# The squares of the first layer's output on VectorE instead of GpSimd

## What is computed

```python
x = x + _L0_xattn_ref(_layernorm(x), ctx_1024, Wq, bq, Wk, bk)
x = x + _L0_ffn_ref(_layernorm(x), w_fc, w_proj)
x = x + _L1_xattn_ref(_layernorm(x), fside, ctx_1024)
x = x + _L1_ffn_ref(_layernorm(x), Wq, keys, e_down, e_up)
```

```python
for s in SHRINKS:                                   # 16 scales
    scale = base * s
    deq = jnp.clip(jnp.round(wb / scale), -QMAX, QMAX) * scale
    err = jnp.sum((deq - wb) ** 2, axis=-1, keepdims=True)
    ... keep the scale of the least err
h = jnp.maximum(turbo_linear(x, w_fc), 0.0)         # 1024 hidden features
return turbo_linear(h * h, w_proj)
```

## Time and profile before

| | us |
|---|---|
| median of 3 runs | 459.7 |
| lowest and highest | 458.96 and 460.38 |
| the profiled execution | 458.2 |
| its span in the trace | 456.4 |

### The profile page before, as it was taken

How to read it: one execution, slowest core, us unless ns; L and a number is a source line. 1 busy time by engine, 2 the same in 40 slices (tenths; PEclk the granted TensorE clock), 3 DMA queues, 4 the chain that set the end, 5 groups by cost and what they waited for, 6 DMA issues and landing times.

```text
span 456.4 us, 6956 instructions
## 1 busy us (share of the span) xinstructions
PE 374.5 (82%) x2510; PEld 283.6 (62%) x2510; DVE 360.9 (79%) x878; ACT 248.4 (54%) x371; POOL 196.8 (43%) x211
## 2 busy tenths in 40 slices
PE   2987897599799988988388679978799878789486
PEld 1554664244345448987267568867688667688475
DVE  4998699958986956267947977698969799999991
ACT  4789959789788880136555254675475645012000
POOL 2355844479889993000011441353523325414220
PEclk9998999989989998998759968999999999979799
DMA  9910000000000004000000000000000000000000
GB/s 264 362 53 2 0 1 0 0 2 0 0 2 0 0 2 159 27 2 0 0 2 1 0 1 1 1 12 1 13 0 14 1 1 14 1 13 0 2 24 11
DMA packets 11138, 11.32 MB, mean 25 GB/s; under 512 B 608, under 2 KB 10592, under 8 KB 11104
## 3 DMA queue, kind: packets, MB, share of 16 engines
q1 hardware_dynamic: 11104, 10.88, 7.4%
HBM read 9.83 MB, written 1.05 MB: 24 GB/s over the span
## 4 chain that ended last, share of the span: by engine, by line
DVE 38%; PE 35%; ACT 13%; issue 9%; POOL 4%; DMA 1%; DVEq 0%; POOLq 0%; ACTq 0%
PE pair L728 6%; PE pair L559 5%; DVE arena L1480 5%; PE pair L697 5%; POOL arena L332 3%; PE pair L519 3%; PE pair L715 3%; PE pair L668 3%; PE pair L497 2%; PE pair L526 2%; DVE arena L1223 2%; DVE arena L1477 1%; DVE arena L1495 1%; PE pair L397 1%; DVE i L1422 1%
## 5 line engine op out<-in xcount | busy, mean ns | idle before, releaser
L332 POOL TENSOR_TENSOR arena<-arena 128x512 f32<-128x512 f32 x64 | 91.0, 1432 | 52.0 <-ACT arena L930 21.5
L697 PE MATMUL pair<-arena,EDT 128*128 128x256 f32 x256 | 59.5, 384 | 3.0 <-ACT arena L1063 3.0
L728 PE MATMUL pair<-EU,arena 128*128 128x256 f32 x256 | 57.8, 380 | 2.8 <-DVE arena L1502 1.6
L1223 DVE TENSOR_REDUCE arena<-arena 128x16 f32<-128x512 f32 x64 | 42.7, 679 | 20.2 <-POOL arena L332 20.1
L519 PE MATMUL pair<-QP,nidentr 128*128 128x512 f32 x144 | 47.6, 456 | 12.5 <-ACT arena L930 9.9
L369 POOL TENSOR_TENSOR arena<-arena,ctxT 128x2048 bf16<-128x2048 bf16 x8 | 34.8, 4351 | 46.9 <-DVE arena L1471 39.6
L697 PEld LDWEIGHTS pair<-arena,EDT 128*128 128x128 f32 x256 | 47.7, 191 | 9.9 <-ACT arena L1063 3.6
L728 PEld LDWEIGHTS pair<-EU,arena 128*128 128x128 f32 x256 | 47.9, 190 | 9.2 <-DVE arena L1495 3.1
L715 PE MATMUL pair<-arena 128*128 128x64 bf16 x768 | 30.4, 203 | 18.8 <-DVE arena L1495 9.4
L519 PEld LDWEIGHTS pair<-QP,nidentr 128*128 128x128 f32 x144 | 27.3, 203 | 24.4 <-issue 16.6
L1063 ACT ACTIVATE arena<-pair 128x512 f32<-128x512 f32 x32 | 18.7, 595 | 42.0 <-PE pair L697 41.9
(11 more groups left out here) (196 smaller groups left out, 686.1 us busy)
## 6 DMA issues: line engine op xcount, KB each, us to landing
arena<-in_L_ffn_e_down_dram SPq DMA_DIRECT2D x1, 2048.0 KB, 12.2
EU<-in_L_ffn_e_up_dram SPq DMA_DIRECT2D x1, 2048.0 KB, 8.1
arena<-in_L_ffn_w_fc_dram SPq DMA_DIRECT2D x2, 512.0 KB, 5.3
X<-in_x_dram SPq DMA_DIRECT2D x1, 1024.0 KB, 6.0
arena<-in_L_ffn_w_proj_dram SPq DMA_DIRECT2D x1, 1024.0 KB, 13.7
GUW<-in_fside_BxS2xS_dram SPq DMA_DIRECT2D x1, 1024.0 KB, 11.4
out_dram<-arena SPq DMA_DIRECT2D x8, 128.0 KB, 1.7
CTX<-in_ctx_dram SPq DMA_DIRECT2D x1, 512.0 KB, 5.0
```

Source lines behind the costliest of these rows:

```text
L332: pool.tensor_tensor(qf(g), sq[:, :, 0:32], sq[:, :, 32:64], ALU.add).then_inc(s["folded"], 1)
L697: last = pe.matmul(bk2(4 + i % 2)[:, r, :], EDT[:, k, at:at + P], xT4[:, b % 2, k, :], start=(k == 0), stop=(k == 1))
L728: last = pe.matmul(bk2(7)[:, n, :], PR[:, n, e, :], EU[:, e, :], start=(e == 0), stop=(e == EROWS - 1))
L1223: dve.tensor_reduce(err[:, g // NS % 2, :, g % NS], qf(g), AX.X, ALU.add).then_inc(s["reduced"], 1)
```

## The change

`square_hidden` is taken out of GpSimd's program and put into VectorE's, with the same operands and the same semaphores. In VectorE's loop it stands in iteration 31 + 2i behind `sum_error` of unit 28 + 2i and ahead of `choose`, `quantise`, `dequantise`, `prepare` and `scale_weights` of the same iteration.

```diff
@@ GpSimd's program
-            def square_hidden(i):
-
-                m, half = i // 2, i % 2
-                pool.wait_ge(s["f1_e"], i + 1)
-                pool.tensor_tensor(h2T[:, m, half * 512:half * 512 + 512], hr[:, i % 2, :], hr[:, i % 2, :],
-                                   ALU.mult).then_inc(s["hsq"], 1)
-
...
                 if g % NS == 12 and g // NS + 1 < NCH:
                     split(g // NS + 1)
-                if g - 2 in FFN1_UNIT:
-                    square_hidden(FFN1_UNIT[g - 2])
@@ VectorE's program
+            def square_hidden(i):
+
+                m, half = i // 2, i % 2
+                dve.wait_ge(s["f1_e"], i + 1)
+                dve.tensor_tensor(h2T[:, m, half * 512:half * 512 + 512], hr[:, i % 2, :], hr[:, i % 2, :],
+                                  ALU.mult).then_inc(s["hsq"], 1)
+
...
                     dve.tensor_reduce(m_w2[:, :], ctxT[:, :].rearrange("p (b t) -> p b t", b=B), AX.X, ALU.max,
                                       apply_absolute_value=True)
+                if g - 2 in FFN1_UNIT:
+                    square_hidden(FFN1_UNIT[g - 2])
                 for b in range(B):
                     if g == 7 + b // 2:
```

## The result

| | median, us | lowest to highest | runs |
|---|---|---|---|
| before | 459.63 | 456.59 to 460.74 | 6 |
| after | 463.92 | 463.23 to 466.18 | 6 |

The changed kernel takes 1.0112 times as long (95% interval 1.0073 to 1.0150), some 4 to 5 us more; a second time, on another chip, it was 1.0155 times (1.0102 to 1.0209). It is slower, as forecast.

A forecast was written before the change was run, and what follows sets the result against it. VectorE was taken to decide when the stage passes 125 and 161 us, GpSimd its end. 3.1 + 5.0 + 1.6 - 1.15 - 1.5 = +7.0 us, added to the median of 459.7: 466.7 us, range 461.0 to 470.0.

The forecast's parts named there:

- What bounds the stage: From 98 to 173 us: VectorE decides when the stage passes 125 and 161 us, GpSimd decides its end.
- The price of one square: On VectorE: 0.69 us plus a turn of up to 1.25 us, waiting out a GpSimd fold.
- the milder rival: Squares take no turn, only 0.69 us and the wait for the relu: +2 us, 461.7 us; chance 0.17.
- First hole, +3.1: TensorE's wait from 122.2 to 125.11 us grows 3.1 us: order 3.2, two squares 1.4, less 1.5 of waits.
- second hole, +5.0: TensorE's 0.26 us wait before 161.17 us grows 5.0 us: choose(2) 2.2 later, squares 1.4, further waits 1.4.
- the third term: Waits from choose to the end of dequantise: 1.5 us fewer at the first hole, 1.4 more at the second.
- the replay: VectorE's queue gone through operation by operation, with turns against GpSimd; gave choose(1) 3.2 us later, choose(2) 2.2.
- The clock, +1.6: Behind the second hole the granted clock falls, so TensorE's sequence takes 1.6 us more; bounds 0 and 1.6.
- The end, -1.15 and -1.5: Before ffn2, the wait for GpSimd's last square shrinks by 1.15 us; full clock in ffn2 saves 1.5.
- No change: As the milder rival, but relief in proportion to GpSimd's operations, 2.4 and 1.5 us saved: 459.9 us; chance 0.07.
- faster: Both holes together grow less than 1.2 us, so the end's 2.65 us gain shows: at best 457.1; chance 0.06.
- Worse: Late VectorE: sums hold folds, folds Squares, squares relus, no clock returns at the end: +10.2, 469.9 us; chance 0.10.

The follow-up runs named there:

- e3_small_pool: Kernel before, with each square on GpSimd cut to 16 of 512 columns, the rest left out; 0.9794 times before, 9.4 us less.
- e6_wait_only: e3_small_pool, but VectorE waits for the relu where the changed kernel has its square, and does nothing there; 0.9909 times before.
- e7_fill: Changed kernel with twelve products of constants on TensorE ahead of the wait for dequantise at both holes; 1.0074 times before, 459.32 us.
- e4_last_three: Kernel before with only the last three squares (13, 14, 15) on VectorE; 0.9939 times before, 455.02 us beside 457.17.
- e11_between: Kernel before with squares 5 to 9 and 13 to 15 on VectorE, the other eight on GpSimd; 0.9951 times before, 454.16 us beside 456.37.

## Why the prediction was right, and where it was off

**What bounds the stage.** Right. TensorE sets the pace between the holes and lost nothing there; all of the loss that the change made stands in the two holes that VectorE releases and behind them, and the gain at the end.

**The price of one square.** Right: 0.67 to 1.63 us, for 0.69 plus up to 1.25. One tensor read twice takes its turn like two; the first condition of the milder rival fell with that. The rule of the Trainium skill ("SBUF — State Buffer", Who interferes with whom) agrees with these runs: with two SBUF inputs a square took up to 1.63 us, and with one of them in PSUM never more than 0.69.

**First hole, +3.1; second hole, +5.0.** Right in sign and place, 1.1 us too large at each (1.99 and 3.92). The order was as reckoned: `choose(1)` started 3.05 us later relative to TensorE (forecast 3.2) and `choose(2)` 2.3 us (2.2). The waits for `dequantise` and `scale_weights` at the first hole were 4.9 and 6.0 us, where I had some 6 and 7. What was mis-sized is the third term, the waits between there and the end of `dequantise`. At the first hole the stretch took 17.81 us in place of 18.87 although it held two more squares, 1.4 us: 2.4 us of waits are gone, where I had 1.5. At the second it took 16.84 us in place of 15.24: with 1.4 for the squares that is 0.2 us of further waits, where I had 1.4. A part of the difference is that the replay laid durations end to end. In the trace an operation of VectorE starts before the recorded end of the one ahead when it has nothing to wait for: 125.35 + 0.69 = 126.04 but the next starts at 125.96. But that is 0.3 to 0.5 us in each stretch (the recorded durations of the first add up to 18.1 us); the rest, some 0.5 us at the first hole and 0.7 at the second, is turns that the replay gave and the trace does not have.

**The three terms of the holes as a sum.** Wrong as an explanation, though the replay as a whole was near. I wrote the first hole as 3.2 (order) + 1.4 (work) - 1.5 (relief), as if each could be taken away by itself. The runs that do take them away move the end of `dequantise` by other amounts, at the first and the second hole (the table above):

| | measured, us | forecast, us |
|---|---|---|
| relief (before to e3_small_pool) | -4.2, -3.4 | -1.5, +1.4 |
| wait for the relu (to e6_wait_only) | +2.7, +2.3 | +3.2, +2.2, with the turn of one square |
| the squares with their turns (to after) | +3.5, +5.0 | +1.4, +1.4 |
| sum | +2.0, +3.9 | +3.1, +5.0 |

The order was well sized. The relief is the step that failed: I counted only the waits that the replay happened to save, 1.5 us at the first hole, and further waits at the second. In place of the 1.5 us it is 4.2. The squares, at 3.5 us instead of 1.4, were too small by nearly as much, and the two errors cancel; that the sum came out as near as it did owes something to this.

**The clock, +1.6.** Right: 2.25 us in the first profile and 1.49 (5.51 less 4.02) in the second. e7_fill shows the cause. I took the price from the sequence behind the first hole, 5.65 us against 4.02; there it comes back at ScalarE's waits and costs nothing, as e7_fill shows. Whether it would be a cost behind the second hole I had not asked. It is: the subtraction of 177.79, which waits for ScalarE there, comes 10.00 us behind the transposes, against 7.75 in the kernel before.

**The end, -1.15 and -1.5.** Right: -1.11 and -1.63, and e4_last_three, which has only this, gained 2.8 us where 2.65 stood in the sum.

**The rest.** At the row where `ffn2` is half through, the sum of the steps was 6.13 us, 5.4 of them without the 0.72 ahead of the first hole; 5.5 are left at the end of the span. The forecast of 7.0 less the 2.2 us of the two oversized holes, plus 0.6 of clock, is 5.4 too. That the end of the span fits as well is luck, since what follows the stage differs by more than this between profiles.

**The rivals.** Milder: out, by the squares' durations. No change and faster: both were right that the relief is larger than in the forecast, and half of the squares in the right places are enough to see it (e11_between). Worse: folds were held by sums (14.3 us of waits), but ScalarE waited 0.6 us for a fold and no more, so this stayed hidden.

## What to carry to other kernels

Before moving an operation from an idle engine to a loaded one, find the waits that the loaded engine releases and count the operations between them: an operation that stands in the engine's own idle time can be free, the same operation in the queue ahead of a release costs its full time and its turns. Where two engines hold each other up, taking work from one speeds the other up. The gain and the price of a move can then both be large and nearly cancel, as here, so that half of the move, in the right places, wins where the whole loses. Moving an operation from ahead of a start to behind it gains nothing if it still lies ahead of the release. And before counting time saved at one place, look for the next wait: here 1.6 us of faster clock behind the first hole came back within 12 us, those behind the second did not.

## What the runs showed of the hardware

Squares with one SBUF operand and one in PSUM ran at 0.67 to 0.69 us beside GpSimd's folds, sixteen times out of sixteen; with both in SBUF up to 1.63 us. A square of 16 columns took up to 0.86 us, against 0.16 at its shortest. TensorE's granted clock stood at 0.50 behind holes of 4.9 and 4.2 us, and in the kernel before behind 2.9 and 2.4 us. It was 1.00 where constant products left 2.29 and 1.61 us of idle time, and behind the 1.30 us in front of `ffn2`, but also behind holes of 2.94 and 2.93 us without products (e4_last_three, e11_between), so that the length of the idle time alone does not decide it here.

What was new to me is how much GpSimd's squares had cost in the kernel before, 9.4 of 457 us, while GpSimd was idle more than half of the span. The list of waits did not show it. Its largest entry, in the kernel before and in e3_small_pool (98 to 176 us), hardly changed:

```profile
DVE arena L1223 <- POOL arena L332: 15.4, 14, 1.7
```

```profile
DVE arena L1225 <- POOL arena L334: 14.2, 15, 1.8
```

Turns lie inside the durations of the operations that take them, and are seen only when the same operation is compared with its shortest.
